# Two of four normalised column blocks scaled into SBUF by VectorE, and the middle stage's scaling moved ahead of its hosted work

## The reference

```python
def _ln(x, g, b):
    mu = jnp.mean(x, -1, keepdims=True)
    var = jnp.var(x, -1, keepdims=True)
    return (x - mu) * jax.lax.rsqrt(var + EPS) * g + b

x   = L0(x, ctx, bias)                       # cross attention, residual, layer norm
h1  = _ln(x, ln1_g, ln1_b)
x   = _attn(h1, h1,  a1_wq, a1_wk, a1_wv, a1_wo, a1_bo, ...) + x   # self attention, 1024 keys
h2  = _ln(x, ln2_g, ln2_b)
x   = _attn(h2, ctx, a2_wq, a2_wk, a2_wv, a2_wo, a2_bo, ...) + x   # cross attention, 64 keys
h3  = _ln(x, ln3_g, ln3_b)
a, g = jnp.split(h3 @ ff_w1 + ff_b1, 2, -1)
x   = a * gelu(g) @ ff_w2 + ff_b2 + x
```

## Time and profile before

| | |
|---|---|
| median of 3 runs | 3287.97 us (3283.62 to 3288.98) |
| the profiled execution's own time | 3277.15 us |
| its span, first to last instruction | 3275.4 us |
| mean granted PE clock | 0.942 of full speed |
| busy: PE, PEld | 2904.6 us (89%), 2120.5 us (65%) |
| busy: DVE, ACT, POOL | 2116.3 us (65%), 1498.1 us (46%), 1771.2 us (54%) |
| DMA | 436.40 MB, mean 133 GB/s |

### The profile page before, as it was taken

How to read it: one execution, slowest core, us unless ns; L and a number is a source line. 1 busy time by engine, 2 the same in 40 slices (tenths; PEclk the granted TensorE clock), 3 DMA queues, 4 the chain that set the end, 5 groups by cost and what they waited for, 6 DMA issues and landing times.

```text
span 3275.4 us, 50801 instructions
## 1 busy us (share of the span) xinstructions
PE 2904.6 (89%) x19712; PEld 2120.5 (65%) x19712; DVE 2116.3 (65%) x3543; ACT 1498.1 (46%) x2178; POOL 1771.2 (54%) x1698
## 2 busy tenths in 40 slices
PE   7677787897899999899889899899989999899998
PEld 6565545566677656667677656666767756666777
DVE  4457695783665596686565587687574588688521
ACT  5332462773333364474333364375334266275321
POOL 3555583884545185485455086386364277376321
PEclk9888657998999899999999999999999999999999
DMA  8754103334543314324353413324353422232444
GB/s 279 237 200 147 59 1 118 121 136 184 168 162 122 127 44 155 127 99 156 125 184 97 161 53 112 124 112 150 131 194 107 148 78 104 84 142 99 160 167 154
DMA packets 199758, 436.40 MB, mean 133 GB/s; under 512 B 94944, under 2 KB 103392, under 8 KB 182368
## 3 DMA queue, kind: packets, MB, share of 16 engines
q1 hardware_dynamic: 199520, 433.15, 37.1%
HBM read 363.38 MB, written 65.54 MB: 131 GB/s over the span
## 4 chain that ended last, share of the span: by engine, by line
PE 56%; POOL 18%; DVE 10%; ACT 6%; issue 6%; DMA 2%; SPq 1%; POOLq 0%; DVEq 0%; ACTq 0%
PE psum L1741 17%; PE psum L1743 15%; PE psum L1742 15%; POOL w1b L1008 7%; PE psum L2037 4%; POOL rec L1003 3%; PE psum L2025 2%; DVE e L1628 2%; ACT psum L1201 2%; PE psum L2051 1%; POOL u_lo L1027 1%; POOL x L922 1%; POOL fw_lo L1015 1%; POOL den L1001 1%; ACT ht_hi L1200 1%
## 5 line engine op out<-in xcount | busy, mean ns | idle before, releaser
L1306 ACT ACTIVATE e<-e,nb 128x1024 f32<-128x1024 f32 x512 | 588.3, 1149 | 326.2 <-DVE e L1628 323.8
L1628 DVE TENSOR_SCALAR_CACHE_REDUCE e<-psum,nscale 128x1024 f32<-128x1024 f32 x512 | 652.4, 1277 | 72.7 <-POOL w1b L1008 56.8
L1008 POOL TENSOR_SCALAR w1b<-e,rec 128x1024 f16<-128x1024 f32 x512 | 572.8, 1119 | 91.4 <-POOL rec L1003 56.2
L1741 PE MATMUL psum<-h_hi,fw_hi 128*128 128x512 f32 x1024 | 456.8, 446 | 31.6 <-DVE h_lo L1393 10.0
L1641 DVE TENSOR_SCALAR w1T<-psum 128x1024 bf16<-128x1024 f16 x512 | 352.1, 688 | 94.2 <-PE psum L2037 91.4
L2037 PE MATMUL psum<-ident,w1b 128*128 128x128 f16 x4096 | 344.1, 232 | 77.4 <-POOL w1b L1008 47.0
L2037 PEld LDWEIGHTS psum<-ident,w1b 128*128 128x128 f16 x4096 | 253.4, 103 | 245.2 <-issue 131.2
L1742 PE MATMUL psum<-h_lo,fw_hi 128*128 128x512 f32 x1024 | 410.2, 401 | 0.0
L1743 PE MATMUL psum<-h_hi,fw_lo 128*128 128x512 f32 x1024 | 409.3, 400 | 0.0
L916 POOL TENSOR_TENSOR rstd<-ve,mhalf 128x1 f32<-128x1 f32 x128 | 88.3, 690 | 403.0 <-DVE ve L1499 403.0
L1491 DVE TENSOR_TENSOR x<-psum,x 128x512 f32<-128x512 f32 x224 | 152.4, 684 | 226.1 <-PE psum L1743 225.3
(11 more groups left out here) (182 smaller groups left out, 6158.9 us busy)
## 6 DMA issues: line engine op xcount, KB each, us to landing
fw_hi<-pieces SPq DMA_DIRECT2D x168, 512.0 KB, 3.3
fw_lo<-pieces SPq DMA_DIRECT2D x168, 512.0 KB, 4.3
w_hi<-kept SPq DMA_DIRECT2D x45, 1024.0 KB, 4.8
w_lo<-kept SPq DMA_DIRECT2D x45, 1024.0 KB, 7.5
mixed<-mixed SPq DMA_DIRECT2D x32, 1024.0 KB, 5.2
fbias<-in_fside_Bx16xSxS SPq DMA_DIRECT2D x64, 256.0 KB, 3.1
unsplit<-in_L_xattn_ff_w SPq DMA_DIRECT2D x24, 512.0 KB, 5.1
pieces<-fw_hi SPq DMA_DIRECT2D x24, 512.0 KB, 2.6
```

The source lines that it names most:

```text
L1008: pool.tensor_scalar(w1b[u % NH][:], e1[u % NE][:], rec1[:, u % 8:u % 8 + 1], HALF, ALU.mult, ALU.add).then_inc(w1_ready.sem, 1)
L1306: act.activation(e1[s % NE][:], e1[s % NE][:], ACT.Exp, bias=nb1[:, s % NE:s % NE + 1], scale=-1.0, accum_out=sum1[:, s % 8:s % 8 + 1]).th ...
L1628: emptied_bank(dve.tensor_scalar(e1[s % NE][:], psum[:, i:i + 2, :].rearrange("p i n -> p (i n)"), nscale[:, 0:1], LARGEST, ALU.mult, ALU.min,
L1741: pe.matmul(o, s_hi, m_hi, start=first, stop=False)
```

## The change

Of the four blocks of a layer norm, blocks 0 and 1 are treated as before. For blocks 2 and 3 DVE reads the bank, and writes z*g+b in fp32 to SBUF, into the parts `z[:, 2]` and `z[:, 3]` whose rows PE has already transposed (a `tensor_scalar` with two per-partition operands, signal `whole_done`). ACT waits for it, writes only the high part of these blocks and no longer rewrites the bank. DVE's low part of blocks 2 and 3 then subtracts SBUF from SBUF. At the start of a self attention whose region was `z` just before, DVE waits for its own last `low_T` instruction. Besides, in `middle` the h2T work of ACT and DVE now stands ahead of `host(NT + 2)` (slot 6), not behind it.

```diff
+WRITTEN_BACK = 2
...
             def norm_T(kind, n, g, bias, hi):
                 for k in range(KT):
-                    affine((kind, n, k), hi[:, k, :], scale=cols[g][:, k:k + 1], bias=cols[bias][:, k:k + 1])
+                    key = (kind, n, k)
+                    to_column = {"scale": cols[g][:, k:k + 1], "bias": cols[bias][:, k:k + 1]}
+                    if k < WRITTEN_BACK:
+                        affine(key, hi[:, k, :], **to_column)
+                    else:
+                        act.wait_ge(whole_done.sem, whole_done.at(key))
+                        act.activation(hi[:, k, :], bank(bank_of(key)), ACT.Identity, **to_column).then_inc(hi_done.sem, 1)
...
+                norm_T("h2T", n, "L1_xattn_ln2_g", "L1_xattn_ln2_b", ht_hi)
                 for m in range(HG):
                     host(NT + 2 + m)
-                    if m == 0:
-                        norm_T("h2T", n, "L1_xattn_ln2_g", "L1_xattn_ln2_b", ht_hi)
...
-            def low_T(kind, n, hi, lo):
+            def low_T(kind, n, g, bias, hi, lo):
+                for k in range(WRITTEN_BACK, KT):
+                    key = (kind, n, k)
+                    wait_filled(dve, key)
+                    dve.tensor_scalar(z[:, k, :], bank(bank_of(key)), cols[g][:, k:k + 1], cols[bias][:, k:k + 1],
+                                      ALU.mult, ALU.add).then_inc(whole_done.sem, 1)
                 for k in range(KT):
                     key = (kind, n, k)
                     dve.wait_ge(hi_done.sem, hi_done.at(key))
-                    emptied_bank(lo_part(lo[:, k, :], bank(bank_of(key)), hi[:, k, :]), key)
+                    whole = bank(bank_of(key)) if k < WRITTEN_BACK else z[:, k, :]
+                    emptied_bank(lo_part(lo[:, k, :], whole, hi[:, k, :]), key)
...
             def self_attention(n):
+                if n % NC > 0:
+                    wait_emptied(dve, ("h3T", n - 1, KT - 1))
...
+                low_T("h2T", n, "L1_xattn_ln2_g", "L1_xattn_ln2_b", ht_hi, ht_lo)
                 for m in range(HG):
                     host(NT + 2 + m)
-                    if m == 0:
-                        low_T("h2T", n, ht_hi, ht_lo)
```

More of the change, by code:

```diff
@@ L451, in build @@
              + [("a2", n, t) for t in range(NT)] + [("h3T", n, k) for k in range(KT)] for n in ns]) for ks in keys for key in ks])
+        whole_done = signal("whole_done", [(kind, n, k) for ns in batches for kinds in (("h1T",), ("h2T", "h3T"))
+                                           for n in ns for kind in kinds for k in range(WRITTEN_BACK, KT)])
         rounded = signal("rounded", [key for ns in batches for keys in (
@@ L1598, in cross @@
                         outer_norm(n, t + 1)
-                low_T("h1T", n, ht_hi, ht_lo)
+                low_T("h1T", n, "L1_xattn_ln1_g", "L1_xattn_ln1_b", ht_hi, ht_lo)
                 host(A_TAIL + NT)
@@ L1708, in middle @@
                     host(s)
-                low_T("h3T", n, h3_hi, h3_lo)
+                low_T("h3T", n, "L1_xattn_ln3_g", "L1_xattn_ln3_b", h3_hi, h3_lo)
             for b in range(B):
```

## The result

The changed kernel takes 3264.14 us (median of 4 runs, 3261.66 to 3268.94) against 3285.80 us (4 runs, 3282.51 to 3288.98) before: a ratio of 0.9940, 95% interval 0.9927 to 0.9953, which is 15 to 24 us less, 19.7 in the middle. A second set gave 3265.19 (6 runs) against 3282.66 (23 runs), 0.9944 (0.9926 to 0.9963), 18.4 us less. Forecast were 3264.8 us and 23.2 us less. The total is right.

What follows compares the result with a forecast made beforehand. PE, busy 89%, was taken as what counts, with ACT setting the pace in layer norms while PE waits. Place terms summed to 23.2 us saved, from 3287.97 to 3264.8 us; range 3252 to 3280.

Steps and rivals of the forecast that it cites:

- the price of the whole: New DVE instruction writing z*g+b of one block to SBUF: 0.75 us taken, between 0.69 and 1.28.
- the slipped first low part: At h1T, DVE's first low part slips from T + 1.45 to T + 1.7, T being ACT's first instruction.
- h2T of chunks 2 to 7: Gains at h2T: 2.0 us over chunks 2, 4, 6 and 5.2 us over chunks 3, 5, 7.
- h3T of chunks 2, 4 and 6: Self attention behind h3T starts 1.2 us earlier in each of these chunks: 3.6 us gained.
- the row of `z` at 4.71 us: Trace row of a DVE `z` beside a 4.49 us POOL instruction; basis for low parts waiting until POOL's instruction ends.
- A: The port does not hold low parts that long; 30 us saved, 3258 us; chance 0.15.
- B: Chunk 1's stall is not returned, later DMA waits take back 7.4 us; 16 us saved, 3272; chance 0.13.
- D: Nothing comes through, each gain is spent waiting for the next DMA or POOL; 3287 us; chance 0.07.
- Rival C: PE's clock falls where `cross` starts behind h3T in three places, turning gain into loss; 3295 us; chance 0.05.
- h1T at 8.0 us: h1T, chunks 2 to 7: POOL runs nothing, PE waits for every block; 6 x 1.33 = 8.0 us gained.
- chunk 1 at 7.4 us: h2T of chunk 1: with the order changed, PE's 12.6 us gap gives 7.4 us.
- h3T of chunks 1, 3, 5 at -4.0: POOL's 4.61 us addition holds low parts at h3T; losses of 2.0, 1.2 and 0.8 us, together -4.0.

Runs made afterwards that it cites:

- the quarters: Kernel after with each POOL bias addition cut into four 128x512 instructions everywhere: 3257.32 us, ratio 0.9928 to before.
- the term alone: Kernel before with the change in h1T only, h2T in its old place: 3275.87 us, ratio 0.9978 to before.
- the order alone: Kernel before with only the h2T work of ACT and DVE moved ahead of slot 6: 3276.85 us, ratio 0.9982 to before.
- Cheap filler in the wait: Kernel after with eight extra 512-column PE matmuls ahead of h1T's first block: 3260.94 us; with quarters where held too, 3251.87 us.

## Why the prediction was right, step by step

Right, and shown: the price of the whole (0.77 for 0.75) and of the slipped first low part; the steps of h1T at the high clock; h2T of chunks 2 to 7 and h3T of chunks 2, 4 and 6, 10.9 for 10.8 us; a low part from SBUF waits until POOL's instruction ends, by the row of `z` at 4.71 us and not by that of L1571 at 1.14, which the quarters confirm; rivals A, B and D are out. The rule of the Trainium skill, "SBUF — State Buffer", section "Who interferes with whom", by which such a pair of instructions exclude each other, agrees with the trace: 4.73 us for two low parts beside an addition of 4.57. Rival C, the clock that makes the kernel slower, did not come, but its mechanism is there in small.

Sized wrong, h1T at 8.0 us. The step "POOL runs nothing in this time, PE waits for every block: 6 x 1.33" took PE's clock for full in chunks 2 to 7 because it was so in the earlier trace rows. In the two profiles of after it was full in 1 of 12 places, and even in the profile that the forecast was made from it was not full at chunks 4 and 7. Read at PE's 37th matmul behind each of the six waits, before comes there at T + 12.65 in the mean of its two profiles and after at T + 12.39: 1.5 us for the six places in place of 8.0. In the runs the term alone gave 7.2 +/- 4.3, in the stretches of the profiles 1 to 4. That the runs of before lose more than its two profiles show would close this gap; it was not measured and stays open, as do the 6 to 8 us between profiles and runs of the whole.

Sized wrong, chunk 1 at 7.4 us. The gap gave 7.9 at PE's next step, but "so the 12.6 us gap gives 7.4" left out that the lower clock behind the gap, till then hidden by ACT, now falls on work that sets the pace: 1.8 to 2 us lost, 5.9 left in the order alone. The held low parts took more, 3.6 being left with both, 6.2 to 6.3 with quarters (all three with the 0.7 that h3T of chunk 0 was forecast to give). Which wait carries that last part from PE's q2 to the later stretch was not found.

Sized wrong the other way, h3T of chunks 1, 3, 5 at -4.0. The held blocks stood as forecast, and at PE's fourth block the three places lost 3.9 us against the first profile of before and 2.4 against the second, in which PE's clock was down at chunk 5 as well (fourth block at T + 7.70 for 6.21). PE carries 3.5 us of it, in the mean, until 65 us behind T; between there and T + 74 it falls to 2.1. What takes the rest up there was not found. Chunk 0 lost 1.0 us more than forecast; POOL goes from its addition at once to the weights, and its two low parts take 4.02 us.

The profiles have 7 us less than forecast at h1T and 4.5 less at chunk 1, against 2 more at h3T and the 6 to 8 us that they do not locate; and the median of before came 2.2 us below the forecast's base. That the median of after fell within 1 us of the forecast is in good part luck.

## What to carry over

Before moving an elementwise step from PSUM to SBUF on DVE, list POOL's long instructions at that time: here each held such a DVE instruction to its end, and cutting POOL's into shorter ones gave 2 to 8 us back. When a supplier is made faster, ask at which clock the consumer runs: a slow clock that hid behind the supplier now shows. Cheap filler in the wait kept the clock up at all twelve places, and was worth 1 to 4 us by itself. Read the clock at every place that a term is multiplied by, not at one.

## What the runs showed of the hardware

- A DVE `tensor_scalar` with two per-partition operands, PSUM to SBUF, 128x512 f32: 0.80 to 0.81 us each, and in a row they start 0.72 to 0.73 apart; ACT's instructions of that size start 0.66 apart.
- The hold goes both ways. The long addition starts first and keeps its 4.57 us, while DVE's two subtractions go from 1.36 to 4.73. Cut in four it takes 5.0 us where no low part from SBUF is due (h3T of the even chunks: from T - 3.54 to T + 1.46, where the whole one ends at T + 1.05), and 5.95 where two get in between.
- PE's granted clock behind the same wait of 2.20 us, nearly always after some 10 us of matmuls at 1.00, went to the lower level in 26 of 42 places and stayed at the higher one in 16. Before, behind a wait of 2.00 us, it went down in 5 of 12. I had taken the clock of one place for the clock of all six.
